# Sums inverted for two units at once, low halves made by GpSimd, and a batch norm taken two feature blocks at a time

## The reference, cut to what matters

```python
# GAT layer, twice (L0)
e = leaky_relu(a_src[src] + a_dst[dst], 0.2)
ex = exp(e - segment_max(e)[dst]);  s = segment_sum(ex, dst)
alpha = ex / (s[dst] + 1e-16)
out = segment_sum(h[src] * alpha, dst)

# transformer layer, l = 0, 1 (L1)
x = batchnorm(x + attn @ Wo[l].T + bo[l], g1[l], beta1[l])     # over the 1250 nodes
ff = relu(x @ W1[l].T + b1[l]) @ W2[l].T + b2[l]
x = batchnorm(x + ff, g2[l], beta2[l])
```

## Time and profile before

| | us |
|---|---|
| median of 3 runs | 1753.84 (1752.67 to 1754.48) |
| profiled execution | 1749.26 |
| its span, first to last instruction | 1747.5 |
| busy: PE, DVE, ACT, POOL | 1575.3, 1313.4, 1167.5, 40.5 |
| mean granted PE clock (share of full) | 0.956 |

### The profile page before, as it was taken

One profiled execution on the slowest core, in us unless ns is written; L12 is line 12 of the kernel. 1 busy time (PEld: TensorE's weight loads), 2 busy tenths in 40 slices (PEclk: granted clock), 3 DMA queues, 4 the chain that ended last, 5 costly groups with the idle time before them and its releaser, 6 DMA issues. The chain is left out here.

```text
span 1747.5 us, 34978 instructions
## 1 busy us (share of the span) xinstructions
PE 1575.3 (90%) x14122; PEld 1432.3 (82%) x14122; DVE 1313.4 (75%) x2387; ACT 1167.5 (67%) x2120; POOL 40.5 (2%) x53
## 2 busy tenths in 40 slices
PE   6898999999987888789979999998898999999971
PEld 3787899999866777678968898888797888888971
DVE  6995999999469999987257777757723777777577
ACT  3454788888647898886457788873433778887323
POOL 0000000000000000000000000002000000000020
PEclk9999899999997999999989999999898999999995
DMA  5113223200006221204964133004087133200204
GB/s 181 53 57 95 79 70 111 85 30 2 1 5 198 94 85 61 73 17 119 267 167 117 50 80 98 2 2 132 2 185 201 63 77 76 64 2 2 61 1 124
DMA packets 73356, 139.34 MB, mean 80 GB/s; under 512 B 16269, under 2 KB 44773, under 8 KB 71912
## 3 DMA queue, kind: packets, MB, share of 16 engines
q1 hardware_dynamic: 73192, 137.06, 27.9%
HBM read 96.22 MB, written 29.45 MB: 72 GB/s over the span
## 5 line engine op out<-in xcount | busy, mean ns | idle before, releaser
L2096 DVE CUSTOM_DVE_ANT_0 probs_att<-banks,logs_or_y 125x1250 f32<-125x1250 f32 x160 | 233.5, 1459 | 140.3 <-PE banks L2000 139.1
L1028 PE MATMUL banks<-ident,probs_gat 125*125 125x125 f32 x1600 | 214.2, 284 | 51.4 <-ACT probs_gat L1132 51.2
L2056 ACT COPY probs_t_att<-banks 125x375 f32<-125x375 f32 (+1 forms) x480 | 205.2, 532 | 76.2 <-PE banks L2010 76.1
L2048 ACT ACTIVATE probs_att<-probs_att,neg_max_att 125x1250 f32<-125x1250 f32 x160 | 218.4, 1365 | 47.8 <-DVE neg_max_att L2096 47.8
L1028 PEld LDWEIGHTS banks<-ident,probs_gat 125*125 125x125 f32 x1600 | 195.3, 196 | 61.7 <-ACT probs_gat L1132 61.1
L1132 ACT ACTIVATE probs_gat<-probs_gat,neg_max_gat 125x1250 f32<-125x1250 f32 x160 | 213.6, 1335 | 43.2 <-DVE neg_max_gat L1286 42.3
L1286 DVE CUSTOM_DVE_ANT_0 probs_gat<-probs_gat,log_counts 125x1250 f32<-125x1250 f32 x160 | 231.8, 1449 | 0.1
L2010 PE MATMUL banks<-ident,probs_att 125*125 125x125 f32 x1600 | 190.3, 274 | 0.6 <-DVE probs_att L2107 0.6
L2021 PE MATMUL banks<-probs_t_att,v_rows 125*64 125x125 f32 x3200 | 189.5, 272 | 0.9 <-ACT feature_cols L2061 0.9
L1039 PE MATMUL banks<-h,probs_t_gat 125*125 125x128 f32 x1600 | 189.2, 274 | 0.0
L2010 PEld LDWEIGHTS banks<-ident,probs_att 125*125 125x125 f32 x1600 | 182.8, 190 | 5.4 <-DVE probs_att L2107 1.2
(11 more groups left out here) (245 smaller groups left out, 2882.5 us busy)
## 6 DMA issues: line engine op xcount, KB each, us to landing
a_pair<-a_src_rows SPq DMA_DIRECT2D x46, 625.0 KB, 4.8
q_first<-q_rows SPq DMA_DIRECT2D x12, 1000.0 KB, 11.8
logs_or_y<-log_rows SPq DMA_DIRECT2D x20, 546.9 KB
q_rows<-q_out_qkv SPq DMA_DIRECT2D x40, 250.0 KB, 4.5
q_att<-q_rows SPq DMA_DIRECT2D x8, 1000.0 KB
w_rows<-in_L_gnn_W_dram SPq DMA_DIRECT2D x12, 512.0 KB, 14.3
log_counts<-counts_fr SPq DMA_DIRECT2D x50, 122.1 KB
k_halves<-k_low_qkv SPq DMA_DIRECT2D x20, 250.0 KB, 3.9
```

What stands on the lines that cost most here:

```text
L1028: block_t = pe.transpose(turned(u)[:, i // 2, (i % 2) * P:(i % 2 + 1) * P], probs[:, u % PROBS, i * P:(i + 1) * P], k.ident[0:P, 0:P])
L2048: act.activation(probs[:, u % SLOTS], probs[:, u % SLOTS], ACT.Exp, scale=-1.0, bias=neg_max[:, column(u)], accum_out=sums[:, column(u)]). ...
L2056: act.copy(probs_t[:, u % TURNED, lo:hi].rearrange("p c n -> p (c n)"), turned(u, j)).then_inc(piece_saved, 1)
L2096: dve.tensor_tensor_reduce(probs[:, u % SLOTS], scores, logs[:, t % KEPT], -1.0, -FLOOR, ALU.add, ALU.min, neg_max[:, column(u)]).then_inc ...
```

## The change

In the second attention, safe and invert are issued once for two units, at even n, on a [125, 2] slice; at odd n DVE issues only ramp, mask and copy_out. The first attention keeps its form. The low halves of the next weights move from DVE to a new POOL program of the stage.

In the tail the first norm is split into two halves of two blocks. DVE's last chunk of the projection is written out as gather_first_norm: the statistics of blocks 0 and 1 are taken as soon as these are added, their root, scale and shift are formed between the additions of blocks 2 and 3. ACT normalises blocks 0 and 1 of chunk 0 itself (own_normed) and casts all four; DVE normalises blocks 2 and 3. POOL starts at the first half's shift and waits for the second's before block 2. widen_first takes each input block for both output blocks, block by block, with output block 1 in another PSUM bank.

```diff
+        def _(pool):
+            for c in range(NEXT):
+                pool.wait_ge(next_high_done, c + 1)
+                pool.tensor_tensor(next_w[2][:, c], next_w[0][:, c], next_w[1][:, c].bitcast(F32), ALU.subtract).then_inc(next_low_done, 1)
...
+            def safe_pair(u):
+                both = slice(u % COLUMNS, u % COLUMNS + 2)
+                dve.wait_ge(exp_done, u + 2)
+                dve.tensor_scalar(sums_safe[:, both], sums[:, both], TINY, None, ALU.add).then_inc(sum_safe, 2)
+            def invert_pair(u):
+                both = slice(u % COLUMNS, u % COLUMNS + 2)
+                dve.wait_ge(sum_safe, u + 2)
+                dve.reciprocal(inverse[:, both], sums_safe[:, both]).then_inc(inverted, 2)
...
-                    if live(layer, n - 1):
+                    if live(0, n - 1) and layer == 0:
                         safe(n - 1)
+                    if live(1, n - 1) and n % 2 == 0:
+                        safe_pair(n - 2)
                     if live(layer, n + 1):
                         mask(n + 1)
-                    if live(layer, n - 1):
+                    if live(0, n - 1) and layer == 0:
                         invert(n - 1)
+                    if live(1, n - 1) and n % 2 == 0:
+                        invert_pair(n - 2)
...
-                        if n - NEXT_AT - 2 in range(0, 4 * NEXT, 4):
-                            lower_next((n - NEXT_AT - 2) // 4)
```

```diff
 # tail, TensorE
+            def widen_first():
+                for c in range(C):
+                    pe.wait_ge(low_done, CHUNKS * C + c + 1)
+                    for o in range(F):
+                        total = three_passes(pe, hidden(CHUNKS, o), in_high[:, CHUNKS % 2, c], in_low[:, CHUNKS % 2, c],
...
 # tail, ScalarE
+            def begin_second():
+                deviate_half(0)
+                act.wait_ge(summed, (CHUNKS - 1) * C)
+                act.wait_ge(shift_done, 1)
+                for c in range(C // 2):
+                    act.activation(y[:, c, nodes(0)], y[:, c, nodes(0)], ACT.Identity, bias=shift[:, 0, c:c + 1],
+                                   scale=scale[:, 0, c:c + 1]).then_inc(own_normed, 1)
+                cut_normed(0)
+                deviate_half(1)
+                for c in range(1, C):
+                    cut_normed(c)
 # tail, GpSimd
+                    if s == CHUNKS + 1 and c == C // 2:
+                        pool.wait_ge(shift_done, 2)
 # tail, VectorE
+            def gather_first_norm():
+                s = CHUNKS - 1
+                add(s, 0, bias_o)
+                measure(s, 0)
+                add(s, 1, bias_o)
+                measure(s, 1)
+                spread_half(0)
+                add(s, 2, bias_o)
+                measure(s, 2)
+                shift_half(0)
+                add(s, 3, bias_o)
+                measure(s, 3)
+                spread_half(1)
+                lower_normed(0)
+                lower_normed(1)
+                shift_half(1)
+                dve.wait_ge(shift_done, 2)
+                for c in (2, 3):
+                    dve.tensor_scalar(y[:, c, nodes(0)], y[:, c, nodes(0)], scale[:, 0, c:c + 1], shift[:, 0, c:c + 1],
+                                      ALU.mult, ALU.add).then_inc(first_normed, 1)
+                lower_normed(2)
+                lower_normed(3)
```

More of the change, by code:

```diff
@@ L2170, in hidden, with half @@
             at = (4 + s % 2) * BANK + c * W
+            if s == CHUNKS and c == 1:
+                at = 6 * BANK
             return k.psum[:, at:at + W]
+        def half(h):
+            return slice(h * C // 2, (h + 1) * C // 2)
         @block.sync
@@ L2230, in _ @@
                 project(s)
-            for s in range(CHUNKS, 2 * CHUNKS + 1):
+            widen_first()
+            for s in range(CHUNKS + 1, 2 * CHUNKS + 1):
                 if s < 2 * CHUNKS:
                     widen(s)
-                if s > CHUNKS:
-                    narrow(s - 1)
+                narrow(s - 1)
         @block.scalar
@@ L2312, in cut @@
                 source = att if s < CHUNKS else y
[L2313 to L2315 removed]
+                for c in range(C if s == 0 else 0):
+                    dve.wait_ge(high_done, c + 1)
+                    dve.tensor_tensor(in_low[:, 0, c], source[:, c, nodes(0)], in_high[:, 0, c].bitcast(F32), ALU.subtract
                                       ).then_inc(low_done, 1)
[L2317 removed]
+                if s > 0:
                     dve.wait_ge(high_done, (s + 1) * C)
@@ L2338, in gather, with lower_normed, spread_half @@
                         measure(s, c - 1)
-            def norm(i):
+            def lower_normed(c):
+                dve.wait_ge(high_done, CHUNKS * C + c + 1)
+                dve.tensor_tensor(in_low[:, CHUNKS % 2, c], y[:, c, nodes(0)], in_high[:, CHUNKS % 2, c].bitcast(F32), ALU.subtract
+                                  ).then_inc(low_done, 1)
+            def spread_half(h):
+                for c in range(C)[half(h)]:
+                    dve.wait_ge(measured, (CHUNKS - 1) * C + c + 1)
+                    done = dve.bn_aggr(moments[:, 0, c], stats[:, 0, c].rearrange("p i v -> p (i v)"))
+                done.then_inc(moments_done, 1)
+                dve.wait_ge(moments_done, h + 1)
+                dve.tensor_scalar(spread[:, 0, half(h)], moments[:, 0, half(h), 1], EPS, None, ALU.add).then_inc(spread_done, 1)
@@ new lines, in shift_half @@
+            def shift_half(h):
+                dve.wait_ge(deviation_done, h + 1)
+                dve.reciprocal(inverse[:, 0, half(h)], deviation[:, 0, half(h)]).then_inc(inverse_done, 1)
+                dve.wait_ge(inverse_done, h + 1)
+                if h == 0:
+                    dve.wait_ge(gains_loaded, 96)
+                dve.tensor_tensor(scale[:, 0, half(h)], inverse[:, 0, half(h)], gain[:, 0, half(h)], ALU.mult).then_inc(scale_done, 1)
+                dve.wait_ge(scale_done, h + 1)
+                dve.tensor_tensor(moved[:, 0, half(h)], moments[:, 0, half(h), 0], scale[:, 0, half(h)], ALU.mult).then_inc(moved_done, 1)
+                dve.wait_ge(moved_done, h + 1)
+                dve.tensor_tensor(shift[:, 0, half(h)], beta[:, 0, half(h)], moved[:, 0, half(h)], ALU.subtract).then_inc(shift_done, 1)
@@ L2346, in norm @@
[L2346 to L2353, removed]
@@ new lines, in last_norm @@
+                dve.reciprocal(inverse[:, 1], deviation[:, 1]).then_inc(inverse_done, 1)
+                dve.wait_ge(inverse_done, 3)
+                dve.tensor_tensor(scale[:, 1], inverse[:, 1], gain[:, 1], ALU.mult).then_inc(scale_done, 1)
+                dve.wait_ge(scale_done, 3)
+                dve.tensor_tensor(moved[:, 1], moments[:, 1, :, 0], scale[:, 1], ALU.mult).then_inc(moved_done, 1)
+                dve.wait_ge(moved_done, 3)
+                dve.tensor_tensor(shift[:, 1], beta[:, 1], moved[:, 1], ALU.subtract).then_inc(shift_done, 1)
@@ L2370, in _ @@
             dve.wait_ge(bias_loaded, 16)
-            for s in range(CHUNKS):
+            for s in range(CHUNKS - 1):
                 gather(s, bias_o)
@@ L2376, in _ @@
                     lower_next(0)
-            norm(0)
-            for c in range(C):
-                dve.tensor_scalar(y[:, c, nodes(0)], y[:, c, nodes(0)], scale[:, 0, c:c + 1], shift[:, 0, c:c + 1],
-                                  ALU.mult, ALU.add).then_inc(first_normed, 1)
-            cut(CHUNKS)
+            gather_first_norm()
             cut(CHUNKS + 1)
```

68 lines of the change are left out of this document (34 added, 34 removed).

## The result

The changed kernel takes 1743.62 us in the median of 4 runs (1742.79 to 1745.36), the kernel before, run beside it, 1753.53 (4 runs, 1752.67 to 1754.48): a ratio of 0.9952, 95% interval 0.994 to 0.9963. It is 9.9 us faster, where 10.0 was forecast. The profiled execution took 1743.77, its span 1742.0.

The account below looks back on a forecast made before the run. DVE was taken to set the second attention's pace, and PE's wait for the first low half to bound the tails. 5.0 - 1.8 + 7.5 - 0.7 = 10.0 us off the timed median gave 1743.8 us (8 in 10: 1738 to 1750).

Parts of the forecast that it names:

- Part 1: Second attention: sums inverted in pairs save DVE 0.135 us per pair, 5.0 us gained (bounds 2.5 to 5.4).
- the 37 of 40 supposed: Second attention: only 37 of 40 pairs count, as three lie before DVE's 4.32 us wait for a DMA.
- Part 2: Second attention: four low halves moved to POOL save DVE 0.59 each but hold it 1.05: 1.8 us lost.
- Part 3: Both tails: first norm in two halves starts PE earlier, 7.5 us gained at full clock (bounds 2.3 to 7.5).
- The 4.2 of layer 0: Layer 0's tail: PE ends chunk two at 1217.7, a gain of 4.2 us.
- the 3.3 of layer 1: Layer 1's tail: chunk two starts at 1671.53 instead of 1674.85, a gain of 3.3 us.
- the 0.7 taken off: Tails: 0.7 us deducted from the first norm's gain for time with PE at half clock rate.
- POOL doesn't hold DVE: Rival, second attention: ramp and mask aren't held by POOL's low halves, +4.2 us, so 1739.6; chance 0.12.
- Fed in drops: Rival, both tails: PE keeps the lower clock to chunk two's end, 5.5 us in all, 1748.3; chance 0.14.
- Pairs nothing: Rival, second attention: DVE's saving from pairs turns into waits for ACT or PE, 5.0 us in all, 1748.8; chance 0.09.
- Slower by PE's clock in the second attention: Rival: POOL's holds make PE's feeding uneven and its clock stays low; 8 us slower, 1761.8; chance 0.05.

Follow-up runs that it names:

- run 6: The changed kernel with POOL's four low halves made only after the last mask of the second attention: 1738.55 us, ratio 0.9934 to the kernel before.
- run 8: The changed kernel with eight more two-input POOL instructions (128x512) in the second attention, one every four units: 1751.74 us, ratio 1.0003 to the kernel before.
- run 1: The kernel before with only the second attention's sums inverted for two units at once: 1746.44 us, ratio 0.9966.
- run 2: The kernel before with only the four low halves of the second attention moved to POOL: 1752.83 us, ratio 0.9999.
- run 3: The kernel before with only the first norm of the tail taken in two halves: 1746.11 us, ratio 0.996.
- run 4: The changed kernel with the four low halves back on DVE: 1741.58 us, ratio 0.9938 to the kernel before.
- run 5: The changed kernel as it is, timed again: 1742.86 us, ratio 0.9958 to the kernel before.
- run 9: The changed kernel with eight more POOL instructions in the second attention, each a one-input copy (128x512): 1745.51 us, ratio 0.9958 to the kernel before.
- run 7: As run 6, with DVE in both tails making the second block's low half before the fourth block's norm: 1738.0 us, ratio 0.993 to the kernel before.
- run 10: The changed kernel with eight more two-input POOL instructions of half size (128x256) in the second attention: 1748.39 us, ratio 0.9976 to the kernel before.

## Why the prediction was right

- **Part 1**, 5.0: the rows give 37 x 0.11 = 4.1. What was mis-sized is "should cost the same, since one column already is fixed cost": the addition two columns wide takes 157 ns in the mean of its 40 where one column took 142, and pushes the mask by 0.08 where one column pushed it by 0.05 to 0.06. The wait of 4.3 us for the third head's rows was left as it was (4.4), as the 37 of 40 supposed.
- **Part 2**, -1.8: the hold was taken as 1.05 and measured 1.08; 4 x (0.60 - 1.08) = -1.9. The step said POOL "slips in as soon as DVE is between two long instructions, and DVE stands until it is through"; that is what the rows show, and runs 6 and 8 show it to be the cause.
- **Part 3**, 7.5 less 0.7: 3.45 + 2.45 = 5.9. The 4.2 of layer 0 is 1221.90, the first of narrow in the earlier trace rows, less the 1217.7 planned; it came as 3.45. The lower level that the prediction counts with is the 0.50 of the earlier trace rows, where 25 products took 5.30 us, 0.21 each. One term was misread: the 3.3 of layer 1 is counted from the 28th product at 1674.85, while chunk two began at 1674.51; from there, or to the first of narrow at 1677.30, the same plan gives 3.0. The other 0.8 in layer 0 and 0.5 in layer 1 are steps that came late. The order of the steps came as laid out. PE's first start was 2.47 after the last product, forecast 2.1: ACT began to cut block 0 at 1209.16 and was done at 1209.54, laid out for 1209.2; the norms of blocks 2 and 3 came at 1211.14 (forecast 1211.0) and their low halves were done at 1212.97 (1212.9). Chunk two was complete on POOL only when ACT took it, 1212.81, laid out for 1212.3, and PE began it at 1215.21, laid out for 1214.85. Its products took 3.20 us (to 1218.41), where 24 x 0.117 is 2.81: the clock's fall to 0.50 in layer 0 cost 0.4, in layer 1 it didn't fall, against the 0.7 taken off. In both layers chunk two began 0.4 late, counted from the last projection (7.63 and 7.64 for 7.23).
- **What no step had**: DVE's 1.3 us at 730, and 1.5 us in layer 0's projections, where PE's clock was at 0.97 over the stretch against 1.00 in the earlier trace rows. Terms of the rows: 4.1 - 1.9 + 5.9 - 1.3 - 1.5 = 5.3, the 5.5 between the profiles.
- **Right in part by luck.** I took 10.0 from the median although the terms were made against an execution 4.6 under it, as if that distance stayed. It didn't: the changed kernel's profiled execution lies on its own median. The terms were too high by about 2, and two waits not foreseen took 2.8; the distance of 4.4 made both good. By the mechanism the forecast was 10.0 and the profiles show 5.5.
- **Where the 4.4 come from is open in part.** That PE's clock has to do with it is argued, from a correlation: over the 26 executions of before beside runs 1 to 4, time goes with PE's mean granted clock (correlation -0.88, 1.18 us for each 0.001; mean clock 0.9535, from 0.952 to 0.958). The mean clock is 0.9565 in the changed kernel's four runs, 0.9568 with the pairs alone, 0.9567 with the tail alone, 0.9544 with POOL's part alone. 0.003 at that slope is 3.5 us. What the traces do show is that the place of a low stretch moves code that no edit touched by as much. From the first ramp of the first attention to the first of the second, which is the same code in all kernels, it takes 349.7 to 350.0 us in eight of the twelve profiled executions and 346.6 to 347.4 in four (runs 2, 5, 8 and 9). The eight have the lower clock near 510 us (0.50 or 0.51), the four don't (1.00). Two executions of the changed kernel show it, the first row of its profile above (349.73), the second of run 5 (346.80):

```profile
509.40:512.80 3.40, 3.40 (x9) 2.55 (x9) 1.71 (x3) 1.07 (x2) 0.00 (x0) 0.51 0.02 5
```

```profile
509.40:512.80 3.40, 3.40 (x16) 2.73 (x15) 0.81 (x2) 0.31 (x1) 0.00 (x0) 1.00 0.00 0
```

About half of these 2.9 us lies earlier, in the first attention. The one profile of before is of an execution 3.9 us under that median of 26, and no trace of one at its median exists, while those of runs 1 and 3 lie at theirs. So why an edit of the attention and one of the tail each bring the better mean clock, and why their gains don't add up, no trace shows.
- **Rivals.** POOL doesn't hold DVE: excluded by runs 6 and 8. Fed in drops: seen in part. The clock was low (0.50) in one of the changed kernel's two tails, but rose again at 1215.9, 0.7 us into chunk two; over all nine profiles with the new tail it falls in 14 of 18 tails between the last projection and narrow, and that stretch is longer than 10.9 us in one of them (12.2, run 8). Pairs nothing: excluded by run 1. Slower by PE's clock in the second attention: one place, 1.3 us, that doesn't need POOL's instructions (run 3).

## What to carry to other kernels

Before moving work to GpSimd, ask what VectorE does meanwhile. Where it ran instructions with two SBUF inputs back to back, the work cost it GpSimd's own time less 0.2: 1.08 us against the 0.60 that VectorE would have needed. The long multiplication with one input in the earlier trace rows was held as well (1.69 us, 0.87 in the median); a reduction with one input was not (0.66 beside GpSimd in runs 8 and 9, 665 ns in the mean of four in the kernel before). Put the work where VectorE no longer sets the pace: one wait on the last mask turned a loss of 1.9 us into a gain of 2.4, by the rows; timed are the 4.3 between the two. And before adding a difference to a median, look at how far the profiled execution lies from it: the 15 executions of the kernel before beside runs 5 to 8 spread over 8 us (1747.15 to 1755.19), their mean granted clocks over 0.952 to 0.958, and of the 9.9 us timed here 4.4 stand in no difference between the two profiles.

## What the runs showed of the hardware

- The hold works both ways and is whole: POOL stands through a ramp of 1.50 us, then DVE stands through POOL's 1.27, 0.73 or 0.62 (runs 8, 10 and 9). POOL's duration in a profile includes its standing: 2.55 for work of 1.27. The rows show it for POOL instructions with one input (the copy of run 9) as well as two. The one-input reduction at 675.11 was not held (0.66 us, 665 ns in the mean of four in before), nor did it hold: POOL kept its 0.62.
- Two DVE instructions with an input in PSUM were not held either, as the prediction supposed for the adding. Adding took 0.47 at 1208.00 in the changed kernel, with POOL's norms under way from 1208.18, and 0.48 at 1207.94 without POOL. The mask of stage_attend, which reads PE's banks, kept 1.46 us in before (1.44 to 1.46 over all 160) while POOL's addition lay wholly beside it and kept its 1.28:

```profile
949.23 1.46 DVE L2096 CUSTOM_DVE_ANT_0 probs_att<-banks,logs_or_y 125x1250 f32<-125x1250 f32 x1 [1.02 <-PE banks L2000]
949.34 1.28 POOL L1987 TENSOR_TENSOR x_tile_att<-x_tile_att,bias_rows_att 125x512 f32<-125x512 f32 x1 [22.59 <-DMA x_tile_att<-x_rows]
```

- An operation of DVE on [125, 2] isn't quite as cheap as on [125, 1]: 157 against 142 ns for the addition, 155 against 153 for the reciprocal, in the changed kernel and before (groups by line, the addition first):

```profile
L1291 DVE TENSOR_SCALAR sums_safe_gat<-sums_gat 125x1 f32<-125x1 f32 x80 | 11.4, 142 | 1.0 <-ACT probs_gat L1132 1.0
```

```profile
L1306 DVE TENSOR_SCALAR sums_safe_gat<-sums_gat 125x2 f32<-125x2 f32 x40 | 6.3, 157 | 1.1 <-ACT probs_gat L1132 1.1
```

- The place of PE's lower clock level (0.50 or 0.51 for 1.00) differs between executions of unchanged code. Near 510 us it stands in eight of twelve executions. Between 725 and 732 us it begins in the changed kernel's two profiles (727.8 and 725.4) and in runs 2 (729.4), 3 (730.2), 8 (730.1) and 10 (731.9), and in none of the other six.
